# Moving the second weight rounding and tanh of each quarter behind other work, and the weight loads ahead of the head loads

## The reference

```
x = x + tanh(g_xattn) * attention(layernorm(x), ctx)      # 16 heads, latent keys and values
x = x + tanh(g_ffn)   * ffn(layernorm(x))                 # 512 -> 2048 -> 512

attention: scores = q_r . k_r (512 x 1024 for each head and batch); softmax; times rotated ctx; projections
ffn:       linear_bit(h, w) = act_quant(rmsnorm(h)) @ ternary_quant(w).T
           ternary_quant(w): s = mean|w|;  round(tanh(w / (s + eps))) * arctanh(s)
```

## Time and profile before

| | us |
|---|---|
| median of 3 runs | 665.2 |
| the profiled execution | 665.11 |
| its span | 663.3 |
| TensorE matmul busy | 636.3 (96%) |
| VectorE busy | 543.7 (82%) |
| GpSimd busy | 430.5 (65%) |
| ScalarE busy | 419.3 (63%) |

### The profile page before, as it was taken

The page is one execution under the profiler, slowest core; times in us unless marked ns, Lnnn a source line. Parts: engine busy times, 40 slices in busy tenths (PEclk is TensorE's granted clock), DMA queues, the critical chain, the costliest instruction groups (busy, mean ns, idle before and its releaser), DMA issues. The chain is left out here.

```text
span 663.3 us, 10048 instructions
## 1 busy us (share of the span) xinstructions
PE 636.3 (96%) x2968; PEld 393.1 (59%) x2968; DVE 543.7 (82%) x870; ACT 419.3 (63%) x693; POOL 430.5 (65%) x368
## 2 busy tenths in 40 slices
PE   8799999999999999999999989999998998999997
PEld 7564566666666676667666645565565454445553
DVE  5777887788878897989799878997799987998963
ACT  2564686377657765776566655666566633598875
POOL 4834588667756775667588966675668353686651
PEclk9999999999999999999999999999999999999999
DMA  8208975888598959984998777868578673000001
GB/s 293 72 5 205 278 203 124 230 229 243 117 251 240 235 130 236 253 223 127 227 255 211 197 205 221 208 184 232 158 209 217 178 172 99 0 1 32 17 34 48
DMA packets 45208, 112.79 MB, mean 170 GB/s; under 512 B 11888, under 2 KB 15088, under 8 KB 45040
## 3 DMA queue, kind: packets, MB, share of 16 engines
q1 hardware_dynamic: 43712, 110.01, 62.0%
q10 hardware_dynamic: 1392, 2.29, 1.0%
q0 software_dynamic: 64, 0.00, 0.0%
HBM read 45.16 MB, written 2.10 MB: 71 GB/s over the span
## 5 line engine op out<-in xcount | busy, mean ns | idle before, releaser
L1194 POOL TENSOR_SCALAR E<-E,small 128x1024 f32<-128x1024 f32 x128 | 146.6, 1147 | 158.6 <-DVE small L1853 156.4
L1675 ACT ACTIVATE E<-ps_s,small 128x1024 f32<-128x1024 f32 x128 | 142.5, 1115 | 161.8 <-DVE small L1848 155.7
L1236 POOL TENSOR_TENSOR G_lo<-G,g_hi 128x512 fp32r<-128x512 f32 x130 | 171.0, 1327 | 7.6 <-ACT g_hi L1621 7.2
L1848 DVE TENSOR_REDUCE small<-ps_s 128x1 f32<-128x1024 f32 x128 | 149.4, 1206 | 24.5 <-PE ps_s L1446 24.5
L1858 DVE STREAM_TRANSPOSE E<-E 128x1024 f32<-128x1024 f32 x124 | 152.6, 1232 | 16.5 <-POOL E L1194 16.5
L1621 ACT ACTIVATE g_hi<-G 128x512 fp32r<-128x512 f32 x130 | 77.8, 631 | 0.0
L1342 PE MATMUL ps_b<-b_hi,ctx_hi 128*128 128x512 f32 x128 | 66.6, 520 | 0.5 <-DVE ctx_lo L1814 0.3
L1479 PE MATMUL ps_b<-G,kv 128*128 128x512 f32 x126 | 63.7, 600 | 1.8 <-DMA G<-E 1.8
L1479 PE MATMUL ps_ctx<-G,kv 128*128 128x512 f32 x126 | 64.6, 607 | 0.6 <-POOL kv L1228 0.6
L1446 PE MATMUL ps_s<-k_hi,q_hi 64*128 64x512 f32 x256 | 57.3, 443 | 8.1 <-ACT E L1675 7.1
L619 PE MATMUL ps_s<-wq,q12T 128*128 128x512 fp8e4 x256 | 59.8, 379 | 0.1
(11 more groups left out here) (204 smaller groups left out, 1222.4 us busy)
## 6 DMA issues: line engine op xcount, KB each, us to landing
G<-E SPq DMA_DIRECT2D x496, 128.0 KB, 2.4
w_stage<-in_wffn SPq DMA_DIRECT2D x48, 512.0 KB, 4.1
wo_s<-in_woT SPq DMA_DIRECT2D x8, 512.0 KB, 5.4
wq_s<-in_wq SPq DMA_DIRECT2D x7, 512.0 KB, 5.7
wkcq_s<-in_wkcqT SPq DMA_DIRECT2D x7, 384.0 KB, 3.3
out<-x_sb SPq DMA_DIRECT2D x8, 256.0 KB, 2.0
x_sb<-in_x SPq DMA_DIRECT2D x3, 512.0 KB, 6.9
wqr_s<-in_wqr SPq DMA_DIRECT2D x7, 192.0 KB, 3.4
```

Of the source, the lines that this page charges most:

```text
L1194: nc.gpsimd.tensor_scalar(e, e, rowinv[:, k:k + 1], 1.0, ALU.mult, ALU.mult).then_inc(scaled, 1)
L1236: nc.gpsimd.tensor_tensor(g_tile(w % 2, i, G_lo), tile, high_part(i).bitcast(F32).rearrange("p (t i q) -> p t i q", t=ST, i=4), ALU.subtra ...
L1675: nc.scalar.activation(out, scores, ACT.Exp, bias=negmax[:, k:k + 1], accum_out=rowsum[:, k:k + 1]).then_inc(exp_done, 1)
L1848: nc.vector.tensor_reduce(negmax[:, k:k + 1], ps_s[:, t % 2, :], AX_X, ALU.max, negate=True).then_inc(max_done, 1)
```

## The change

Three edits. The second `tanh_half` of a unit moves from step 3 to step 4 on ScalarE, where it stands behind the high part of the side task of that step and the last `split_high`. The second `round_half` moves on VectorE from its place ahead of the last `turn_blocks` of `u2` to one behind the two `max_tile` of `u3` and the low part of step 6. The two `stage_load` of a unit move on SyncE to right behind `exchange`, ahead of `load_q`, `load_wq` and `load_kr`.

```diff
-SUM_STEPS, TANH_STEPS, ROUND_STEPS = (1, 4), (0, 3), (4, 5)
+SUM_STEPS, TANH_STEPS, ROUND_STEPS = (1, 4), (0, 4), (4, 6)
...
                 if not (variant == "last" and w == 3):
                     exchange(sp, *unit_ahead(p, w, 1))
+                for q, g in halves_loaded(p, w, mode):
+                    stage_load(sp, q, mode, g)
                 if w == 1 and not (variant == "last" or isinstance(p, int) and p == 6):
                     sp.wait_ge(side_done, side_index(p, variant, ("b", 1)) + 1)
                     load_q(sp, p + 2)
...
                     load_kr(sp, p + 2)
-                for q, g in halves_loaded(p, w, mode):
-                    stage_load(sp, q, mode, g)
...
                 low(5)
-                rounded(5)
                 if second:
                     turn_blocks(dve, *u2, 3)
...
                 if w:
                     low(6)
+                rounded(6)
                 if variant == "last":
                     ffn_dve_early(dve, w, 6)
                 if first:
```

## The result

The changed kernel is slower. It takes 674.2 us in the median of 4 runs (672.08 to 675.2), beside 665.15 us (664.93 to 665.3) for the kernel before: ratio 1.0132, 95% interval 1.0106 to 1.0158. A later set of runs on another chip gave 672.61 us for 665.56, ratio 1.0096 (1.0076 to 1.0116). So it loses 7 to 9 us; forecast was a gain of 2.2.

What follows compares the result with a forecast made beforehand. TensorE, busy 96% of the span, was taken as the bound, with at most about 10 us of VectorE-caused stops to gain. 1.1 - 2.8 + 1.7 - 1.1 - 0.8 - 0.3 = -2.2 us: 662.9 from 665.11, range 658.5 to 666.8.

Steps and rivals of the forecast that it cites:

- VectorE's loop: VectorE's list per unit: shorter only by what the moved rounding shortens, 0.4 us per unit, 1.67 us in (5, 0).
- the dearer case in pair 4: Moved rounding in pair 4 beside a GpSimd sum, sharing a port pair: up to 1.7 us more than 0.68.
- ScalarE's edit and (5, 0): High part of k 1.04 us earlier in (5, 0) and (6, 0); with the shorter rounding, 2.8 us less in (5, 0).
- The small stops of pair 4 (1.6) and (5, 0) (2.8): TensorE stops expected to vanish behind the late exchange in pair 4 and at the b and q tasks of (5, 0).
- The start of the exchange: SyncE in (4, 1): exchange begins at 343.4, 3.0 us late; in (5, 1) 3.4 later than 409.81.
- 2.3 us more. I take that: 357.5: Exchange of (4, 1) behind 1600 KB of loads: last landing at 357.5 us, 2.7 us after its reader's 354.82.
- The backlog term: Delay of the exchange by loads issued ahead: 0.75 us of issue plus 1.6 of landing, 2.3 us more.
- rival two: Loads drain slower; exchanges of (4, 1) and (5, 1) land 1.8 us later than forecast, at 359.3 in pair 4: 666.5 us; chance 0.18.
- in w = 3 and w = 0, I cost the late exchange at nothing: Late exchanges in those units hidden by longer units, cost 0; up to 1 us each if that cover is gone.
- a small gain (-0.3): Pair 7: rounding 0.68 in both places, one stop a bit shorter, so 0.3 us less.
- a gain of 2.9: Up to (6, 3): -1.0 for two stops at the end of (5, 3), -1.1 in (6, 0), -0.8 in rest of pair 6.
- Rival one: Late exchange hidden by overlap or an earlier rounding end: -8.2 us, 656.9, or about 658 with 0.4 per exchange; chance 0.17.

Runs made afterwards that it cites:

- the run with 704 KB: Changed kernel, same queue order and waits, but weight loads and `load_wq` in pairs 4 to 6 carry 16 of 128 partitions (weights not right); 660.85 us, ratio 0.9926.
- the SyncE edit alone: Kernel before with only the weight loads moved ahead of the head loads on SyncE, roundings and tanh as before; 665.65 us, ratio 1.0006.
- the fillers: Changed kernel plus 18 matmuls with overwritten output ahead of the value product of (4, 3) and of (5, 3); 670.71 us, ratio 1.0074.
- rounding and SyncE: Changed kernel with the second tanh back at step 3; 674.13 us, ratio 1.0099.
- the best of them: Changed kernel with the second weight load issued by SyncE within the next unit's exchange, behind its fourth DMA; 659.55 us, ratio 0.9908.
- rounding and tanh: Changed kernel with the old order on SyncE, so without the SyncE edit; 662.73 us, ratio 0.9936.
- first load, head loads, second load: Changed kernel with only the second weight load put behind the head loads on SyncE, the exchange last; 663.59 us, ratio 0.9958.
- rounding alone: Kernel before with only the second rounding moved to step 6, old SyncE order, tanh at step 3; 660.41 us, ratio 0.9941.

## Why the prediction was wrong

**VectorE's loop: right.** The last transpose of (4, 1) begins at 343.11 for 343.32; pair 4 itself began 0.2 us later than before. That is 0.4 us less, as worked out, and the second rounding lasts 0.67 or 0.68 us in every unit; the dearer case in pair 4, with GpSimd in its way, did not come.

**ScalarE's edit and (5, 0): right in kind, a little smaller.** Between the scores of (4, 3) and the q task of (5, 0) the lateness shrank from 6.4 to 3.3 us, by 3.1, and the stop of 0.42 us ahead of those scores was gone, 0.4 more. The small stops of pair 4 (1.6) and (5, 0) (2.8) were to give 4.4, so 0.9 is missing. In (5, 0) the stop at the b task is gone, but 0.90 of the 1.60 us at the q task is left. The first rounding of that unit, now 1.25 us, is one term that I did not have.

**The start of the exchange: right.** Forecast 343.4, measured 343.58; for (5, 1) 3.4 later than 409.81 in its own unit's time, and it came at 416.41 in a program some 3 us late.

**The failed step, first half: "2.3 us more. I take that: 357.5".** The backlog term was mis-sized. The issue took no longer (10.16 us for 10.04), so the 0.75 us in it did not come, but the landing took 3.2 us more in the median (5.6 for 2.4), where the term had 1.6: the last DMA, issued at 353.2, landed some 5.6 us later, at 358.8, 1.3 us later than forecast. The row that I took the 2.3 from had 1152 KB ahead of the exchange; here 1600 KB stood there. The landing agrees with what rival two worked out from the drain rate (359.3, less than 0.5 us away), and the run with 704 KB landed in 3.0 us, while the SyncE edit alone, with 1600 KB and no late rounding, landed in the same 5.6. Rival two's condition, a landing 1.1 us later than mine in both pairs, came true, and so did its sign, stops of over 4 us and in other units as well; but its time, 666.5, was still 7.7 us short, for it had the same gap as the forecast:

**The failed step, second half: what a stop of 4 us does.** The prediction costs a stop at its own length. Before, TensorE never stood for over 1.8 us behind an exchange, and the clock was full throughout. In the stops of 4.2 and 4.4 us it fell to 1.2 GHz, and that cost 2.7 us in pair 4 and 2.2 in pair 5 (shown with the fillers). Neither forecast nor rival had it. The Trainium skill ("TensorE: Matmul & The Clock Gate", section "HAM oscillation — how this bites in real kernels") tells of just this: a wait for a DMA that lets the clock fall, so that the next stretch starts slow. The trace agrees (granted clock 0.50 from 358.0 to 364.5 us), and I did not bring the rule to bear. Each profiled stop for G of 3.3 to 4.7 us came with a fall of the clock. Between 1.7 and 2.3 us it goes both ways: stops for G of 1.73 to 2.24 us in pair 7 left the clock full in twelve profiles, one of 1.82 did not (rounding and SyncE), nor did the pair of 1.00 and 1.76 us above. Alone, no profiled stop for G of 1.5 us or less brought it down.

**The third failed step: "in w = 3 and w = 0, I cost the late exchange at nothing".** In pair 7 the exchange of (7, 0) begins at 519.13 for 508.94, 10.2 us later in a program that is 7.6 late, behind weight loads that themselves waited for a rounding, and its DMAs land in 5.0 us in the median for 4.0; the stops that follow (1.26 us, and 1.76 for an exponential) raise the lateness from 7.6 to 9.2. In (6, 3) there is another 0.45. The prediction gave this the sign of a small gain (-0.3).

**The sum again.** From -2.2 to +9.2 is 11.4 us. At the first reader in (4, 3) the changed kernel was 1.4 us later than forecast; the clock there made 2.7; the gains up to the q task of (5, 0) were 0.9 smaller. The landing in (5, 3) was 1.3 later. Up to (6, 3) a gain of 2.9 was forecast and the lateness grew by 0.3, of which the second fall of the clock is 2.2; and pair 7 made 1.9. 1.4 + 2.7 + 0.9 + 1.3 + 3.2 + 1.9 = 11.4. 4.9 of the 11.4 us are the clock, 2.7 the two landings.

**Rival one**, that the exchange is hidden, is false for the changed kernel, but its gain is what the kernels with the moved rounding and another queue order show, in part: 0.9908 to 0.9958. Its 657 to 658 us is 1.6 to 2.6 under the best of them (659.55).

**Left open.** Why the executions of one kernel with the moved rounding can differ by up to 11 us where those of the kernel before differ by 2. The clock behind the stops of pair 7 is a part of it. In the profiled run of rounding and tanh the first scores product and the first product at L1342 behind it stand 4.58 us apart; in the profile of "first load, head loads, second load", where the clock stayed full there, they stand 3.01 apart. That makes 1.6 us, but the two runs of rounding and tanh that lie furthest apart differ by 10.7. The rest is not shown, since only the profiled executions show their stops.

## What to carry to other kernels

When work is moved to a later step, follow the semaphore that it releases to the queue that waits for it, and list everything behind that wait, bytes included: here an edit that costs nothing alone and one that gains 4 to 5 us alone cost 7 to 9 us together. Time in hand hides most of either delay alone, and is there only once. Price a new stop of TensorE with the slow stretch behind it as well as its length, and give it two prices, one in which the clock holds and one in which it falls; here a stop of 1.8 us had now the one and now the other. A load that may be late belongs behind what must be early, within a long issue of DMAs if need be.

## What the runs showed of the hardware

- TensorE, at the full granted clock until then, fell to 1.2 GHz at a single stop of 4.2 us and stayed there until 5.7 us after the value product (3.4 to 4.3 at three other stops of 4.2 to 4.6 us, in two profiles of the same kernel); 18 filler products in the stop held it at 2.4 GHz and saved 2.7 us at that place. The stop of 1.47 us with fewer bytes left it at 2.4. Stops for G of 1.79 and 1.82 us at the same place in pair 7 left it at 2.4 in one kernel and were followed by 1.2 in another.
- With 1600 KB of loads issued within the 2 to 2.5 us ahead of them, block DMAs from SBUF to SBUF of 128 KB landed 5.6 us after issue in the median; with 1152 KB, 4.0 in the kernel before and 5.0 in the changed one (pair 7); with 704 KB, 3.0; with one weight load of 512 KB, 2.3 to 2.7 ("rounding alone", "rounding and tanh").
- A rounding's length goes with what GpSimd does beside it: the second one lasted 2.35 us beside a sum of 2.39 and 0.67 to 0.68 us in its new place in every unit, in (4, 1) with GpSimd idle but for the first 0.1 us; the first one of (5, 0) and (6, 0) went from 0.68 to 1.25 us, without an edit to it, beside two splits of 2.99 us in all.
